# Adjacency masks made during the first normalisation, T's rows turned on TensorE, expert chunks of 1024 tokens

## The reference

```python
x = x + gnn0(layernorm(x), adj, adj, ...)   # 3 attention heads + two GRU cells
x = x + ffn0(layernorm(x)[None], ...)[0]    # 1 shared + 8 private experts, F = 512, top 2, gelu
x = x + gnn1(layernorm(x), adj, ...)        # adj @ (bilinear form of x), relu
x = x + ffn1(layernorm(x)[None], ...)[0]    # 8 experts, F = 256, top 2, relu
```

## Time and profile before

| | |
|---|---|
| three runs | 2173.95, 2177.00, 2177.86 us; median 2177.0 |
| profiled execution | 2179.8 us; its span 2178.0 us |
| PE busy | 1838.2 us (84% of the span) |
| DVE busy | 1678.1 us (77%) |
| ACT busy | 1406.2 us (65%) |
| POOL busy | 201.6 us (9%) |
| moved by DMA | 313.89 MB |

### The profile page before, as it was taken

One profiled execution on the slowest core, in us unless ns is written; L12 is line 12 of the kernel. 1 busy time (PEld: TensorE's weight loads), 2 busy tenths in 40 slices (PEclk: granted clock), 3 DMA queues, 4 the chain that ended last, 5 costly groups with the idle time before them and its releaser, 6 DMA issues.

```text
span 2178.0 us, 30551 instructions
## 1 busy us (share of the span) xinstructions
PE 1838.2 (84%) x9101; PEld 878.2 (40%) x9101; DVE 1678.1 (77%) x1760; ACT 1406.2 (65%) x1799; POOL 201.6 (9%) x154
## 2 busy tenths in 40 slices
PE   4222484599999999999998899999998899997997
PEld 4211131244444444444444544444454344463332
DVE  3555416788898999998857598888968988855898
ACT  1677004787788788787634466767656877626875
POOL 0000001100010101100244000000006900000000
PEclk6555698799999999999998799999999999988999
...
GB/s 145 429 427 359 0 81 166 189 149 156 165 154 151 168 155 150 179 145 154 159 126 0 45 74 39 39 39 42 36 21 116 0 347 428 342 39 90 100 83 77
DMA packets 79575, 313.89 MB, mean 144 GB/s; under 512 B 13958, under 2 KB 14438, under 8 KB 69494
## 3 DMA queue, kind: packets, MB, share of 16 engines
...
HBM read 297.88 MB, written 15.08 MB: 144 GB/s over the span
## 4 chain that ended last, share of the span: by engine, by line
PE 43%; DVE 8%; issue 3%; ACT 1%; DMA 1%; POOL 0%; DVEq 0%; SPq 0%; ACTq 0%; POOLq 0%
PE psum L943 9%; PE psum L953 9%; PE psum L1025 8%; PE psum L893 7%; DVE hidp L1399 2%; PE psum L1003 2%; DVE xT L1421 2%; DVE yT L1418 2%; PE psum L917 1%; PE psum L919 1%; PE psum L765 1%; PE psum L931 1%; DVE prod L1458 1%; PE psum L760 1%; PE psum L771 1%
## 5 line engine op out<-in xcount | busy, mean ns | idle before, releaser
L593 ACT ACTIVATE ss<-KR,dpt 128x1024 bf16<-128x1024 int16 x384 | 413.1, 1138 | 110.9 <-DVE pl L1291 110.2
L893 PE MATMUL psum<-ph,Tt 128*128 128x512 bf16 x1536 | 416.3, 380 | 6.6 <-DVE pl L1291 6.6
L669 ACT ACTIVATE hid<-psum,fB 128x512 f32<-128x512 f32 x416 | 271.1, 685 | 150.0 <-PE psum L943 110.5
L953 PE MATMUL psum<-hidp,fW 128*128 128x512 bf16 x1248 | 293.5, 381 | 19.4 <-DVE hidp L1399 15.1
L943 PE MATMUL psum<-hTp,fW 128*128 (+1 forms) x1248 | 297.6, 385 | 3.9 <-ACT mk L683 2.8
L1399 DVE TENSOR_TENSOR hidp<-hid,hidp 128x512 bf16<-128x512 f32 x416 | 268.5, 687 | 27.0 <-DVE xT L1421 10.4
L1288 DVE TENSOR_TENSOR ph<-ss,Ahi 128x3072 bf16<-128x3072 bf16 x128 | 228.3, 1784 | 58.4 <-PE psum L893 58.2
L893 PE MATMUL psum<-pl,Tt 128*128 128x512 bf16 x768 | 228.9, 380 | 0.0
L1291 DVE TENSOR_TENSOR pl<-ss,Alo 128x3072 bf16<-128x3072 bf16 x128 | 227.2, 1775 | 0.0
L893 PEld LDWEIGHTS psum<-ph,Tt 128*128 128x128 bf16 x1536 | 150.0, 98 | 190.0 <-issue 6.5
L953 PEld LDWEIGHTS psum<-hidp,fW 128*128 128x128 bf16 x1248 | 117.9, 98 | 181.9 <-issue 41.0
...
## 6 DMA issues: line engine op xcount, KB each, us to landing
Ar<-in_adjT SPq DMA_DIRECT2D x32, 2048.0 KB, 12.9
Ab<-in_adjT SPq DMA_DIRECT2D x128, 512.0 KB, 4.2
A<-in_adjT SPq DMA_DIRECT2D x32, 2048.0 KB, 11.1
Tt<-T_d SPq DMA_DIRECT2D x128, 256.0 KB, 2.6
mB<-mk_d SPq DMA_DIRECT2D x128, 256.0 KB, 7.6
...
```

The source lines that it names most:

```text
L593: last = nc.scalar.activation(ss[s % 2][:, h, :], KR[:, h, rb * RB:(rb + 1) * RB], ACT.Sigmoid, scale=STEP, bias=dpt[:, ds(t * HEADS + h, 1)])
L669: nc.scalar.activation(hid[j % HB][:, :], psum[:, j % HB, :], func, bias=fB1[:, j:j + 1]).then_inc(act_done[k], 1)
L893: last = nc.tensor.matmul(psum[:, 2 * h + q, :], Tt[s % AS][:, h, w, :], mv[:, q * CH:(q + 1) * CH], start=fresh and k == 0, stop=False, s ...
L953: last = nc.tensor.matmul(psum[:, HB + e % dn, :], fW[1][x][:, j * P:(j + 1) * P], hidp[j % ring][:, y, :], start=(f == 0 and w == 0), sto ...
```

## The change

Three edits, independent of each other.

**Masks and first normalisation.** SP issues the first four adj tiles right behind xT. The tiles go in the order `turn`, 16 to 31 and then 0 to 15. DVE's and ACT's programs alternate between steps of the normalisation and masks: nine masks stand ahead of the copies into uvs. Only hT is spilled, between the 16th and the 17th adj tile, and the transfer of adj's diagonal moves behind the pass.

**T build.** hn_d and hn2 are gone. PE turns the tile of hT in fp32 into the last 128 columns of the tile's PSUM bank ahead of the three matmuls; wm4 has a fourth column of ones, and DVE's L1250 covers 512 columns in place of 384. ACT's L578 is gone. PE now waits for t_lo as well, four tiles back.

**Expert layers.** 4 chunks of 1024 tokens (NW, CW) in place of 8 of 512. Each weight tile serves two matmuls of 512. A hidden tile takes two PSUM banks, so up has 2 places in place of 4 and down 2 in place of 3 or 4. hid has 4 buffers, of 1024; hidp has 9 in layer 0 in place of 12. The masks are 8 buffers of 1024, waited for in pairs; `down` waits for hid_lo tile by tile.

The core of the diff:

```diff
+        turn = [(t + NT // 2) % NT for t in range(NT)]
@@ sync
+            for n in range(MS):
+                sp.dma_start(Ar[n][:, :], adj[turn[n] * P:(turn[n] + 1) * P, :]).then_inc(m_in[n], 16)
             sp.dma_start(gwTt[:, :], a["gatWT"]).then_inc(gat_in, 16)
             sp.dma_start(ga[:, :, :], a["gatA"]).then_inc(gat_in, 16)
+            for n in range(MS, NT):
+                if n == NT // 2:
+                    sp.wait_ge(ln_done, 2)
+                    sp.dma_start(hT_d, hT[:, :]).then_inc(spilled, 16)
+                sp.wait_ge(m_neg, n - MS + 1)
+                sp.dma_start(Ar[n % MS][:, :], adj[turn[n] * P:(turn[n] + 1) * P, :]).then_inc(m_in[n % MS], 16)
-            sp.dma_start(hn_d, hn[:, :, :].rearrange("p t f -> p (t f)")).then_inc(spilled, 16)
-            sp.dma_start(hn2[:, :], hn_d).then_inc(att_in, 16)
@@ scalar, first normalisation
+            squares(0)
+            negative(0)
+            deviation(0)
+            squares(1)
+            negative(1)
+            deviation(1)
+            negative(2)
+            turned_back(0)
+            negative(3)
+            negative(4)
+            turned_back(1)
+            for n in range(5, NT):
+                negative(n)
@@ vector, first normalisation
+                centred(0)
+                centred(1)
+                mask(0)
+                variance(0)
+                mask(1)
+                normed(0)
+                mask(2)
+                variance(1)
+                mask(3)
+                normed(1)
+                mask(4)
...
+            mask(5)
+            mask(6)
             dve.wait_ge(uv_ps, 1)
...
+            mask(7)
+            mask(8)
             dve.wait_ge(uv_ps, 2)
@@ tensor, T build
-                        pe.wait_ge(t_mul, n + 1)
+                    pe.wait_ge(t_lo, n + 1)
+                    pe.wait_ge(t_mul, n + 1)
+                    nc.tensor.transpose(psum[:, s, HEADS * P:], hT[:, t * P:(t + 1) * P], ident)
@@ tensor, expert layers
-                            last = nc.tensor.matmul(psum[:, j % HB, :], fW[0][x][:, j * P:(j + 1) * P],
-                                                    hTp[y][:, nlast(q)], start=(w == 0), stop=(w == 2))
+                            for b in range(2):
+                                last = nc.tensor.matmul(psum[:, j % 2 * 2 + b, :], fW[0][x][:, j * P:(j + 1) * P],
+                                                        hTp[y][:, ds(q * CW + b * CH, CH)], start=(w == 0),
+                                                        stop=(w == 2))
@@ scalar, expert layers
-                act.sem_inc(act_done[k], HB)
-                ring = (12, 8)[k]
+                act.sem_inc(act_done[k], 2)
+                ring, hold = (9, 8)[k], (3, 4)[k]
-                    nc.scalar.activation(hid[j % HB][:, :], psum[:, j % HB, :], func,
+                    nc.scalar.activation(hid[j % HB][:, :], flat[:, j % 2 * CW:j % 2 * CW + CW], func,
```

More of the change, by code:

```diff
@@ L512, in ln_scalar, with negative, squares @@
         def ln_scalar(act):
-            for hf in range(2):
+            def negative(n):
+                act.wait_ge(m_mask, n + 1)
+                nc.scalar.activation(Ar[n % MS][:, :], Ar[n % MS][:, :], ACT.Relu, scale=-1.0,
+                                     accum_out=negs[:, turn[n]:turn[n] + 1]).then_inc(m_neg, 1)
+            def squares(hf):
                 act.wait_ge(ln_centred, hf + 1)
@@ L540, in _ @@
             ln_scalar(act)
-            with act.Fori(0, NT // MS) as i:
-                for s in range(MS):
-                    act.wait_ge(m_mask, MS * i + s + 1)
-                    nc.scalar.activation(Ar[s][:, :], Ar[s][:, :], ACT.Relu, scale=-1.0,
-                                         accum_out=negs[:, ds(MS * i + s, 1)]).then_inc(m_neg, 1)
             act.wait_ge(nsign_ok, 1)
@@ L690, in ffn_scalar @@
                 for j in range(HB, nE * nF):
-                    hidden(NC - 1, j)
+                    hidden(NW - 1, j)
             ffn_weights(0, *FFN0)
@@ L810, in _ @@
                 pe.wait_ge(m_mask, n + 1)
-                sums(lambda c, w: keep[:, n * N + c:n * N + c + w],
-                     uvs[:, n:n + 1, :, :].rearrange("p o a b -> p (o a b)"), m_sum)
+                sums(lambda c, w: keep[:, turn[n] * N + c:turn[n] * N + c + w],
+                     uvs[:, turn[n]:turn[n] + 1, :, :].rearrange("p o a b -> p (o a b)"), m_sum)
             pe.wait_ge(neg_rows, 1)
@@ L860, in _ @@
             with pe.Fori(0, nsign) as sg:
-                with pe.Fori(0, NT // TS) as i:
-                    for s in range(TS):
-                        n = sg * NT + TS * i + s
-                        pe.wait_ge(t_mul, n + 1)
-                        for w, (x, y) in enumerate(((0, 0), (0, 1), (1, 0))):
-                            last = nc.tensor.matmul(psum[:, s, 0:HEADS * P], hTs[x][:, ds((TS * i + s) * P, P)],
-                                                    gwb[y][:, :], start=(w == 0), stop=(w == 2))
-                        last.then_inc(t_ps, 1)
+                for t in range(NT):
+                    n, s = sg * NT + t, t % TS
+                    pe.wait_ge(t_lo, n + 1)
+                    pe.wait_ge(t_mul, n + 1)
+                    nc.tensor.transpose(psum[:, s, HEADS * P:], hT[:, t * P:(t + 1) * P], ident)
+                    for w, (x, y) in enumerate(((0, 0), (0, 1), (1, 0))):
+                        last = nc.tensor.matmul(psum[:, s, 0:HEADS * P], hTs[x][:, t * P:(t + 1) * P],
+                                                gwb[y][:, :], start=(w == 0), stop=(w == 2))
+                    last.then_inc(t_ps, 1)
             pe.sem_inc(a_mm, AS)
@@ L1044, in inverse_root, with mask, centred @@
                 return V.tensor_tensor(stat[:, 4, t], stat[:, 4, t], stat[:, 5, t], ALU.mult)
+            def mask(n):
+                t = turn[n]
+                blk = Ar[n % MS][:, t * P:(t + 1) * P]
+                dve.wait_ge(m_in[n % MS], n // MS * 16 + 16)
+                V.tensor_tensor(blk, blk, offd, ALU.mult).then_inc(m_diag, 1)
+                dve.wait_ge(m_diag, n + 1)
+                V.tensor_scalar(keep[:, t * N:(t + 1) * N], Ar[n % MS][:, :], 0.0, None, ALU.is_gt,
+                                saturate=False).then_inc(m_mask, 1)
             def ln_vector():
-                for hf in range(2):
+                def centred(hf):
                     t = slice(16 * hf, 16 * hf + 16)
                     ps = flat[:, hf * N // 2:(hf + 1) * N // 2].rearrange("p (t f) -> p t f", f=P)
-                    wide = [P, 16, P]
                     dve.wait_ge(ln_turned, hf + 1)
@@ L1406, in high, with weighted @@
                         lo(j + 1)
[L1408 to L1411 removed]
+                def weighted(q, e, f):
+                    xq, p = xT[:, wide(q)], e - (nE - NE)
+                    if p >= 0 and p % 2 == 0:
+                        dve.wait_ge(mB_in[p // 2], (k * NW + q + 1) * 32)
                     dve.wait_ge(down_done[k], q * nE + hold + e + 1)
[L1413 to L1414 removed]
+                    y = flat[:, (2 + e % 2) * CW:(3 + e % 2) * CW]
+                    if p < 0:
                         f.link(V.scalar_tensor_tensor(out=xq, in0=y, scalar=fB2[:, e:e + 1], in1=xq,
@@ L1433, in ffn_vector @@
                     high(0, e)
-                with dve.Fori(0, NC // 2 - 1) as i:
-                    for half in range(2):
-                        chunk(2 * i + half, i, half, True)
-                chunk(NC - 2, NC // 2 - 1, 0, True)
-                chunk(NC - 1, NC // 2 - 1, 1, False)
+                with dve.Fori(0, NW - 1) as q:
+                    chunk(q, True)
+                chunk(NW - 1, False)
             lt_vector(0, lambda: low_weights(0, *FFN0))
```

157 lines of the change are left out of this document (71 added, 86 removed).

## The result

Four timed runs of the changed kernel took 2133.41 to 2138.74 us, median 2137.5; the kernel before took 2173.95 to 2177.86 beside them, median 2176.1. The ratio is 0.9818, with a 95% interval of 0.9802 to 0.9834: 38.6 us less. The profiled execution took 2138.74, its span is 2136.9, against 2178.0 before. The forecast was 2135.4, or 2138.2 for a profiled execution.

The account below looks back on a forecast made before the run. It took adj loads to bound the mask pass, PE the first expert layer, DVE the T build and second layer. −27.7 + 4.5 + 5.4 − 23.8 = −41.6 gave 2135.4 us (2138.2 profiled), range 2119 to 2153.

Parts of the forecast that it names:

- Part A: Mask pass: making masks during the first normalisation brings the last adj tile to 183.2 us from 210.9, −27.7.
- part B: T build: DVE's scaling of 512 columns instead of 384 adds 0.135 a tile, plus 0.3 for the first transpose: +4.5.
- The first rival: Mask pass: early adj loads delay xT to near 29 us, the saving falls to about −10, total 2153; 4%.
- The second rival: Mask pass: comes near its best, −36, total 2127, the long gap hanging on the u, v matmuls alone; 12%.
- The upper bound of 198: Mask pass, slow case: each of the first 13 loads runs alone at 7.2 us, ending at 198, −13.
- Part C, first layer: First expert layer, PE-bound: later start, third-tile waits, vanished gaps and a longer end sum to +5.4.
- The wait at the third tile: First layer's up: PE waits 1.44 for ACT to empty the first tile, against 1.295 of matmuls: +0.15, 35 times, +5.3.
- the third rival: PE waits for ACT at every hidden tile of the first layer, DVE still limits the second: about 2158; 12%.
- (3): First expert layer: the gaps of 1.9 us seen in PE's window go, −1.9.
- Part C, second layer: Second expert layer: PE becomes the limit at 5.18 an expert and the stall on masks goes, −23.8.
- The fifth rival: Second layer: DVE's steps stay at 5.74 as its waits grow with the tile; +5 there, total 2164; 5%.
- the fourth rival: Expert layers: new short waits bring PE's clock down; slower if over 202 matmuls run at 1.2 GHz; 3%.

Follow-up runs that it names:

- e1: The changed kernel with the expert chunks put back to 512 tokens, masks and T build as changed: 2154.6 us.
- e3: The changed kernel with up and down of the first expert layer alternating on PE in halves of two tiles: 2134.4 us.
- e4: The changed kernel with the first four adj loads issued only once xT has landed: 2137.4 us.
- e7: The changed kernel with the router's exp on ACT behind the second hidden tile instead of the fourth: 2125.0 us.
- e5: The changed kernel with DVE's wait for the u, v matmuls, and the copies behind it, moved from after mask 8 to after mask 10: 2135.3 us.
- e8: The changed kernel with the T build edit undone: hn written to DRAM behind hT's spill, read back, put into T by ACT: 2140.5 us.
- e2: The kernel before with only the expert chunks widened to 1024 tokens, masks and T build as before: 2161.0 us.
- e10: The changed kernel with e5's later wait, e7's early exp, and up/down halves except at each chunk's first expert: 2123.9 us.

## Why the prediction was right

The time was 2.1 us from the forecast, and the terms were near, but that they add up so closely is in part luck. Part A fell 2.5 short in the profile shown, the first layer cost 2.8 more than reckoned and the stretch behind it 2.2 more, a term that the sum did not have; against that part B came out 0.9 and the second layer 2.9 better, and the stages that no part touches were 3.3 shorter. One cost was missing altogether, the table loads.

- **Part A, −27.7.** After: −25.2 (192.2 against 217.4). In e1, e3, e4 and e7, with the same part, −26.8 to −27.5: the profile shown is at the long end of a spread. Load 13 was forecast at 88.0 and came at 91.0 (87.5 in e1), DVE's wait for u, v at 6 us and was 3.67, since it started later. The first rival (xT delayed) falls with e1 and e4. The second rival rested on a gap that hangs on the u, v matmuls; e5 gives it 2 of the 8 us at most. The spill of hT, 6.6 in the sum, shows as 4.8 at load 16 and at most 1.2 at load 15; the last load is 0.8 late, with the moved transfer of adj's diagonal issued ahead of it, which the sum had at nothing. The upper bound of 198 is one load short: 13 loads at 7.2 and 19 at 4.92 give 203, −8 in place of −13. The forecast doesn't hang on it.
- **Part B, +4.5.** +3.6 after, +4.4 in e1: 1.26 to 1.29 a tile against 1.28. e8 shows the other side, which the sum had only as a load that no longer stood in the way: the write would have cost 4.9 at its place, and no more than 7.
- **Part C, first layer, +5.4.** Counted from the first `up` to n: 392.7 before, 400.9 after, +8.2 (e2: +8.7). The start took 3.9 more, 4.6 were forecast. The wait at the third tile is 0.15, 35 times, as forecast (the three terms given for its 1.44 add up to 1.42, which would make it 0.13), and e3 removes it; the third rival, a wait at every tile, doesn't occur. The gaps of (3) did go: they were the two waits at the turns of DVE's loop (steps of 6.50 and 6.10 in place of 5.18, 2.2 us). What failed in (3) is that the sum put nothing in their place. With two places in PSUM each of the three table loads in the loop reaches PE, 3.8, and e7 takes these waits away. So −1.9 became +1.6, the 3.5 us by which restart to n was off (+4.3 measured, +0.8 in the sum).
- **Part C, second layer, −23.8.** From r to the end 230.6 before, 203.9 after: −26.7. PE is the limit at 5.18, no wait for masks remains, and the last DVE row ends 165.2 behind the restart, 165.8 reckoned. That waiting for two masks at a time took the stall away is read from the trace; no run parts it from the wider step. The start cost 4.0, not 5.6, and the rest was 1.3 better. The fifth rival falls.
- **The clock.** 1.00 in both layers, in the first with a wait at each expert: the fourth rival doesn't occur. Nor do the swings that the Trainium skill (TensorE: Matmul & The Clock Gate, "A second HAM failure mode: psum-queue depth-cycling") has for a PE that idles briefly between groups while it cycles through PSUM banks. Where the clock did fall was behind the layer, at the wait of 2.73 for DVE (1.66 before); the 16 matmuls there took 7.10 before, 8.80 after, 10.15 in e10. The sum had the longer last weighing at its 1.1, without this; it is most of the 2.2 by which n to r grew.
